# Two transformer layers on one core: engine queues ordered stage by stage, and operation by operation

## The reference

```
for l in (0, 1):
    x = x + attention_l(layernorm(x), ctx, ctx, mask_l)      # softmax over 128 keys, 16 heads
    h = layernorm(x)
    if l == 0:  x = x + bitlinear(silu(bitlinear(h, Wg)) * bitlinear(h, Wu), Wd)
    else:       x = x + sum over the 2 best experts e of w_e * (relu(h @ W1[e].T + b1[e]) @ W2[e].T + b2[e])
```

## Time and profile before

| | us |
|---|---|
| Median of 3 runs (lowest, highest) | 238.72 (238.11, 239.03) |
| The profiled execution | 239.16 |
| Its span | 237.3 |
| PE matmul busy, 2097 instructions | 201.5 |
| PE weight loads busy | 166.0 |
| DVE busy, 573 instructions | 169.5 |
| ACT busy, 377 instructions | 134.3 |
| POOL busy, 232 instructions | 110.6 |

### The profile page before, as it was taken

How to read it: one execution, slowest core, us unless ns; L and a number is a source line. 1 busy time by engine, 2 the same in 40 slices (tenths; PEclk the granted TensorE clock), 3 DMA queues, 4 the chain that set the end, 5 groups by cost and what they waited for, 6 DMA issues and landing times.

```text
span 237.3 us, 5951 instructions
## 1 busy us (share of the span) xinstructions
PE 201.5 (85%) x2097; PEld 166.0 (70%) x2114; DVE 169.5 (71%) x573; ACT 134.3 (57%) x377; POOL 110.6 (47%) x232
## 2 busy tenths in 40 slices
PE   0467299988675799898999999999899999999993
PEld 0245077866353577675779789897779979999992
DVE  1541974899999999999888998679756364625335
ACT  2242028685445465585959666567567738366560
POOL 6997022352475746423244562845262460482531
PEclk9999999999999689999999999999999999999998
DMA  6999044244003147040404002340400400000000
GB/s 203 356 397 201 1 88 41 53 90 91 0 3 62 28 88 91 0 91 15 82 0 76 15 4 38 64 91 11 91 0 3 91 12 4 0 14 11 14 0 22
DMA packets 39442, 15.09 MB, mean 64 GB/s; under 512 B 34163, under 2 KB 38515, under 8 KB 39158
## 3 DMA queue, kind: packets, MB, share of 16 engines
q1 hardware_dynamic: 38982, 14.00, 27.3%
q10 hardware_dynamic: 432, 0.72, 0.9%
HBM read 5.80 MB, written 0.52 MB: 27 GB/s over the span
## 4 chain that ended last, share of the span: by engine, by line
PE 49%; DVE 33%; DMA 4%; issue 4%; POOL 4%; SPq 2%; ACT 2%; DVEq 0%; ACTq 0%; POOLq 0%; another core or an unknown queue 0%
PE ps_B L705 11%; PE ps_A L720 10%; DVE mx L924 7%; PE ps_O L648 4%; PE ps_A L591 4%; PE ps_A L593 3%; PE ps_Q L637 3%; PE ps_B L606 3%; PE ps_B L608 3%; DMA wf_sb<-in_wd 3%; PE ps_P L628 2%; POOL yc L553 2%; DMA kblk<-kst 2%; DVE z L988 2%; PE ps_O L657 2%
## 5 line engine op out<-in xcount | busy, mean ns | idle before, releaser
L924 DVE TENSOR_REDUCE mx<-ps_A 128x4 f32<-128x512 f32 x64 | 41.9, 681 | 10.0 <-PE ps_A L593 9.5
L806 ACT ACTIVATE probs<-ps_B 128x512 f32<-128x512 f32 x64 | 36.9, 608 | 12.3 <-PE ps_B L608 11.9
L816 ACT ACTIVATE hid<-ps_B,b_sb 128x128 f32<-128x128 f32 x128 | 35.6, 383 | 12.7 <-PE ps_B L705 12.6
L591 PE MATMUL ps_A<-m_b,id_b 128*128 128x512 bf16 x64 | 25.9, 405 | 11.7 <-DVE mx L924 8.8
L705 PE MATMUL ps_B<-mxT,w_sb 128*128 128x128 f32 x256 | 33.5, 279 | 0.1
L720 PE MATMUL ps_A<-w_sb,hid 128*128 128x128 f32 x256 | 31.1, 275 | 0.4
L720 PEld LDWEIGHTS ps_A<-w_sb,hid 128*128 128x128 f32 x256 | 31.1, 192 | 0.6
L705 PEld LDWEIGHTS ps_B<-mxT,w_sb 128*128 128x128 f32 x256 | 30.6, 192 | 0.3 <-issue 0.2
L443 POOL TENSOR_SCALAR hv<-mv 128x1 f32<-128x1 f32 x32 | 7.3, 229 | 50.3 <-DVE mv L899 50.2
L553 POOL TENSOR_TENSOR yc<-yc 128x512 f32<-128x512 f32 (+2 forms) x21 | 17.2, 818 | 27.0 <-DVE yc L1052 25.9
L452 POOL TENSOR_SCALAR xh<-x_sb,mv,ry 128x128 f32<-128x128 f32 x32 | 26.1, 816 | 3.5
(11 more groups left out here) (128 smaller groups left out, 399.8 us busy)
## 6 DMA issues: line engine op xcount, KB each, us to landing
w_sb<-in_m1T SPq DMA_DIRECT2D x1, 1024.0 KB
w_sb<-in_m2T SPq DMA_DIRECT2D x1, 1024.0 KB
ctx_sb<-in_ctxT ACTq DMA_DIRECT2D x1, 512.0 KB, 5.0
m_i<-in_mask SPq DMA_DIRECT2D x1, 512.0 KB, 6.8
m0T_i<-in_mask0T SPq DMA_DIRECT2D x1, 512.0 KB, 7.5
out_y<-out_sb SPq DMA_DIRECT2D x8, 64.0 KB, 1.6
x_sb<-in_x SPq DMA_DIRECT2D x1, 448.0 KB, 5.5
wf_sb<-in_wg SPq DMA_DIRECT2D x1, 256.0 KB, 6.0
```

The lines of the kernel that those rows point to most:

```text
L591: pe.matmul(o[:, :].rearrange("p (h k) -> p h k", h=4), id_b[:, :], m, start=True, stop=False)
L806: ins = act.activation(probs[:, n % 2, 4 * i:4 * i + 4, :], psum("exp", n, i)[:, :].rearrange("p (h k) -> p h k", h=4), ACT.Exp, scale=ATT ...
L816: ins = act.activation(hid[:, b % 2, 4 * i + c, :], psum("z", b, i)[:, c * P:(c + 1) * P], ACT.Relu, bias=b1_sb[:, 4 * i + c:4 * i + c + 1])
L924: ins = dve.tensor_reduce(mx[:, n % 2, 4 * i:4 * i + 4], psum("max", n, i)[:, :].rearrange("p (h k) -> p h k", h=4), AX.X, ALU.max)
```

## The change

The plan orders operations where it ordered stages. Each helper's chain is cut into named steps (on DVE: st, ag, nm, rk, rq, m1, mr, m2, m3, rd, at, fs, fa, fn, q0 to qc, xr, xq, h0 to h3, hr, hq, lg to c5), each with a semaphore of its own. A step waits for those steps whose results or slots it needs, and between two steps of one unit the queue can hold steps of others. The plan's durations become pairs (`TIME`): the distance to the next step and the time to the end; a transpose of keys has 2.5 and 4.5. `START`, `BIAS` and two places in the unit order are new.

Keys and values are one product ("kv") that needs only the context, in bank X; the queries are another ("q"), in bank P. The 128x128 step of every layer norm moves from POOL to DVE (nm, fn). In the split of the maxima, the second part is computed from the maxima and the first part and no longer copied from the rest. The weights' sums (ws), product for the means (wm), three ternary steps for each of the three matrices (wa, wb, wc), the bias parts (five bp) and masks (mk, m1) are steps of their own. The loads: the context in two parts, keys' weights first; the feed-forward weights ahead of the mask of layer 1; a semaphore for each. POOL's clearing of all staging slots comes ahead of the first norm. The rest of the arithmetic and of the tiles stays.

```diff
-UNIT_ORDER = ((0, 0), (0, 1), (0, 2), (0, 3), (0, 4), (0, 5), (1, 0), (0, 6), (1, 1), (1, 2), (0, 7),
+UNIT_ORDER = ((0, 0), (0, 1), (0, 2), (0, 3), (0, 4), (0, 5), (0, 6), (1, 0), (0, 7), (1, 1), (1, 2),
               (1, 3), (1, 4), (1, 5), (1, 6), (1, 7))
 ATTENTION = (
-    ("pe.xT", 1, "pool.norm"),
+    ("dve.st", 1),
+    ("dve.ag", 1, "dve.st"),
+    ("pool.pw", 1, "dve.ag"),
+    ("dve.nm", 1, "pool.pw"),
+    ("pe.kv", 1),
+    ("act.kh", 1, "pe.kv"),
+    ("act.v", 1, "pe.kv"),
+    ("dve.rk", 1, "act.kh", "act.v"),
+    ("pool.km", 1, "dve.rk"),
+    ("pool.kl", 1, "pool.km"),
+    ("sp.ks", 1, "pool.kl"),
+    ("pe.xT", 1, "dve.nm"),
     ("act.xT", 1, "pe.xT"),
-    ("pe.qkv", 1, "act.xT"),
-    ("act.qkv", 1, "pe.qkv"),
-    ("dve.qkv", 1, "act.qkv"),
-    ("pool.low", 1, "dve.qkv"),
-    ("sp.ks", 1, "pool.low"),
-    ("pe.qs", 1, "pool.low"),
+    ("pe.q", 1, "act.xT"),
+    ("act.qh", 1, "pe.q"),
+    ("dve.rq", 1, "act.qh"),
+    ("pool.qm", 1, "dve.rq"),
+    ("pool.ql", 1, "pool.qm"),
+    ("pe.qs", 1, "pool.ql"),
...
+ONCE = (
+    ("dve.ws", 3),
+    ("pe.wm", 1, "dve.ws"),
+    ("dve.wm", 1, "pe.wm"),
+    ("dve.wa", 3, "dve.wm"),
+    ("dve.wb", 3, "dve.wa"),
+    ("dve.wc", 3, "dve.wb"),
+    ("pool.m1", 1),
+    ("dve.bp", 5),
 )
...
-LATENCY = 0.26
-LANDING = 3.5
+LATENCY = 0.1
+SAME = 0.03
 PATIENCE = 0.01
-START = (7, -55.6, 91.8, 80.2, 94.6, 137, 2.4, -27.2, -19.8, -42.4, 46, 26.4, 126.8, -60.8, 159.6, -19)
-
+START = (-36, -22, 2, -46, 42, 62, 14, 36, 63, 53, 102, 61, 36, 4, 44, -80)
...
+        def after(eng, step, u, i=None):
+
+            eng.wait_ge(done[step], u * counts[step] + (counts[step] if i is None else i + 1))
+
+        def ends(ins, step):
+            ins.then_inc(done[step], 1)
...
+            def power(k, b, step, u):
+
+                pool.tensor_scalar(hv[:, k, b, 0:1], mv[:, k, b, 1:2], EPS, None, ALU.add).then_inc(var_ready, 1)
+                small[0] += 1
+                pool.wait_ge(var_ready, small[0])
+                ends(pool.tensor_tensor(ry[:, k, b, :], hv[:, k, b, 0:1], half[:, :], ALU.pow), step)
...
+                if name == "nm":
+                    after(dve, "pool.pw", n)
+                    if n >= 2:
+                        after(dve, "pe.xT", n - 2)
+                    ends(dve.tensor_scalar(xh[:, n % 2, :], x_sb[:, b, :], mv[:, 2 * l, b, 0:1], ry[:, 2 * l, b, :],
+                                           ALU.subtract, ALU.mult), "dve.nm")
...
+                if name == "m2":
+                    st, m, rest = head_max(n)
+                    after(dve, "dve.m1", n)
+                    ends(dve.scalar_tensor_tensor(out=st[:, :, :, 1], in0=m, scalar=-1.0, in1=st[:, :, :, 0],
+                                                  op0=ALU.mult, op1=ALU.subtract), "dve.m2")
...
+                if name == "wa":
+                    after(dve, "dve.wm", 0)
+                    ends(dve.tensor_scalar(wf_sb[:, i, :], wf_sb[:, i, :], wf_inv[:, i:i + 1], ROUND,
+                                           ALU.mult, ALU.add), "dve.wa")
...
+                if name == "bp": bias_part(i)
```

More of the change, by code:

```diff
@@ L38 @@
 GROUPS = H // 2
-PAIR = 2 * DH
 PARTS = 6
@@ L130 @@
 )
[L132 to L146, removed]
-)
@@ L149 @@
[L149 to L157, removed]
@@ new lines, in _ @@
+                if name == "qs":
+                    after(pe, "pool.ql", n)
+                    stack("qs", n, ROWS)
+                if name == "max": maxima_scores(n, i)
+                if name == "qb":
+                    after(pe, "dve.m3", n)
+                    stack("qb", n, MROWS)
+                if name == "exp": shifted_scores(n, i)
+                if name == "pv":
+                    after(pe, "act.v", n)
+                    after(pe, "act.exp", n)
+                    wait_free(pe, "pv", n)
+                    if n == 0:
+                        pe.wait_ge(bank_zero, 1)
+                    o = psum("pv", n)
+                    for h in range(H):
+                        j = h % 4
+                        mm = pe.matmul(o[32 * j:32 * j + DH + 1, (h // 4) * P:(h // 4 + 1) * P],
+                                       v_sb[:, n % KSLOTS, h, :], probs[:, n % 2, h, :], start=True, stop=True)
+                    ends(mm, "pe.pv")
@@ new lines, in _ @@
+                if name == "oT":
+                    after(pe, "act.pv", n)
+                    wait_free(pe, "oT", n)
+                    o = psum("oT", n)
+                    for g in range(4):
+                        mm = pe.transpose(o[:, g * P:(g + 1) * P], oT_sb[:, n % 2, g * P:(g + 1) * P], ident)
+                    ends(mm, "pe.oT")
+                if name == "aT":
+                    after(pe, "dve.at", n)
+                    turn("aT", n, attn[:, n % 2, :, :].rearrange("p h d -> p (h d)"), ident)
@@ new lines, in _ @@
+                if name == "z":
+                    if b == 0 and i == 0:
+                        pe.wait_ge(s_moe, 80)
+                    if i == 0:
+                        after(pe, "act.mxT", b)
+                    wait_free(pe, "z", b, i)
+                    for c in range(4):
+                        mm = pe.matmul(psum("z", b, i)[:, c * P:(c + 1) * P], w1_sb[:, 4 * i + c, :], mxT[:, b % 2, :],
+                                       start=True, stop=True)
+                    ends(mm, "pe.z")
@@ new lines, in _ @@
+                if name == "y":
+                    if b == 0 and i == 0:
+                        after(pe, "dve.bp", 0)
+                        pe.wait_ge(ones_ready, 2)
+                    wait_free(pe, "y", b, i)
+                    o = psum("y", b, i)
+                    pe.matmul(o[:, :], rows3[:, :], b2_p[:, i * 512:(i + 1) * 512], start=True, stop=False)
+                    after(pe, "act.z", b, 2 * i + 1)
+                    for c in range(8 * i, 8 * i + 8):
+                        e = c // 2 - 4 * i
+                        mm = pe.matmul(o[:, e * P:(e + 1) * P], hid[:, b % 2, c, :], w2_sb[:, c, :],
+                                       start=False, stop=(c == 8 * i + 7))
+                    ends(mm, "pe.y")
```

1302 lines of the change are left out of this document (682 added, 620 removed).

## The result

The changed kernel takes 222.57 us (median of 4, 222.05 to 223.34), the kernel before 238.88 (median of 4, 238.11 to 239.15): a ratio of 0.9325, 95% interval 0.9284 to 0.9366. The gain is 16.3 us; 19.0 were forecast.

A forecast was written before the change was run, and what follows sets the result against it. Three stages were seen: a waiting start, a middle where DVE is fuller, an end where PE is. 237.3 - 6 - 12 - 1 = 218.3 us of span, plus 1.86 less 0.44 gives 219.7 us; range 206 to 234.

The forecast's parts named there:

- The middle: From 34 to 123 us, where DVE is the fuller engine: shrinks by 12 us, bounds 0 and 21.
- uncovered waits: DVE in the middle stage: 116 waits of 0.12 us, all covered by other units' steps, 13.9 us less.
- norm steps: Last step of each normalisation moves from POOL to DVE: some 15 in the middle, 3 us more, bounds 2 and 4.2.
- the bias block: Five bias steps run as one block from 69.60 us, then PE waits: splitting them gains 3, inside the middle's 12.
- the prediction's third rival: DVE's pitch doesn't fall, chained steps costing the same with or without waits between: 237 us, chance 0.05.
- The start: Before 34 us, where PE and DVE are idle half of the time: gain 6 us, bounds 1 and 8.
- the block that leaves the path: Start: nine ternary steps and the means, 4.2 and 0.7 us, done in DVE's idle time: 4.9 us gained.
- an earlier landing of the keys: Start: first key transpose lands at 20.3 us instead of 21.4, between 18.6 and 21.4: 1.1 us gained.
- The end: From 123 us, where PE is already full: gain 1 us from 2 us of pauses, bounds 0 and 2.
- Keys apart from queries: Keys and values in bank X, queries in P: cost 0, any gain inside the middle's 0 to 21.
- The rival "slower": Queues run in order and PE stands waiting for late key transposes, sixteen waits of 1.5 us: 243.7 us, chance 0.12.
- the marks that the prediction named: Signs in the new trace by stage: step distances, busy totals, transpose issue, PE waits, first expert product near 105 us.

The follow-up runs named there:

- e_stage: Changed kernel with the steps of each chain standing together again in VectorE's queue, all other queues unchanged: 246.47 us.
- e_blocks: Changed kernel with the nine ternary steps packed together and the five bias steps packed together in VectorE's queue: 228.54 us.
- e_hole: Changed kernel with the third weight sum, the product for the means, the means and nine ternary steps ahead of the first maximum: 221.46 us.
- e_early: Changed kernel with the five loads of expert weights issued behind the fifth key transpose, not ahead of the first: 217.24 us.
- e_early2: Changed kernel with the five loads of expert weights issued after the second key transpose, not ahead of the first: 216.92 us.
- k_tied: Changed kernel with keys and values of a unit computed only behind the transposed queries' input, all queues planned again: 235.56 us.
- k_stage: Changed kernel with the planner itself keeping the VectorE steps of a chain together, all five queues planned again: 242.94 us.
- k_pool: Changed kernel with both 128x128 norm steps back on GpSimd, queues planned again with a limit on how far key products run ahead: 239.26 us.
- e_both: Changed kernel with the edits of e_early2 and e_hole together: 219.5 us.
- e_twice: Changed kernel with each of the 32 norm steps done twice on VectorE, first into an unread spare tile, orders unchanged: 230.2 us.

## Why the prediction was right, and where it was not

**The middle: the length right, its split only in part.** 12 us were forecast: 10.9 less content on DVE (13.9 of uncovered waits less 3 of norm steps), and 1 less idle time. By the same PE prices as in the prediction, the pauses between 34 us and the first expert product went from 21 to 8.7 us: 12.3. The mechanism is there: 0.12 to 0.13 us from start to start per wait, in the rows of both kernels, and 12.9 us of DVE busy time that come back in e_stage. But the sum came out by two misses that offset each other. Between 34 us and the first expert product DVE's busy time fell from 78.9 to 72.9 us, by 6.0 and not by 10.9 (the stage doesn't hold quite the same work: some ternary steps are in it, and 35 "max" reductions instead of 39); its idle time fell from 10.1 to 2.7 us, by 7.4 and not by 1. That the length was hit this closely is luck. What filled the idle time, no run takes apart. One part is the bias block: in the kernel before PE waits 2.94 us behind it and is then busy 6.1 us in 6.8 us at half clock, both gone in the kernel after, and with the two blocks packed again it costs 6.0 us (e_blocks), where the prediction gave 3.

A norm step takes 0.36 (xh) or 0.40 us (fh), not 0.28, and is followed after 0.25 (28.09 to 28.34) instead of 0.2: 3.8 instead of 3, within its bounds. Chains packed again cost 20 to 24 us; the 12 are a net figure against a kernel whose queues were planned for its stages.

The Trainium skill ("VectorE: DVE Perf Modes", section "The DRAIN you can't avoid"), whose rule is the prediction's third rival, would have packing cost nothing. By the measurement it costs 23.9 us, of which 12.9 are on DVE itself. The measurement decides. The same section adds that a next operation that isn't held starts earlier, and with that the trace agrees: 0.06 to 0.13 us behind steps of 0.14 to 0.21.

**The start: one term right, one mis-sized.** Forecast 6 us (bounds 1 to 8): 4.9 for the block that leaves the path, 1.1 for an earlier landing of the keys. By the same prices PE had done 7.3 us of its work at 34 us before (counted from its instructions; the prediction has 8) and 9.4 after: 2 us. The 4.9 are there: the fourth "max" piece starts 7.8 us behind the first before (21.48 to 29.25) and 2.7 us after (23.43 to 26.08), 5.1 less. They didn't come as foreseen, by the nine steps filling DVE's idle time, for the third weight sum stands behind the first maxima in the queue; they came because the steps stand behind all four maxima. e_hole, where they do fill it, adds 1.1 us.

The term that failed is the landing: 20.3 forecast, between 18.6 and 21.4, and 23.4 measured (21.8 in the earliest execution with these loads and this order), so that 1.1 us of gain became 2 us of loss. Both of its bounds took SP's loads as issued when they were before, the last at 11.31. In the kernel after single issues took up to 1.33 us, the second of the two large expert loads went out at 11.75 instead of 9.56, and the last load at 13.35. The keys land 11.8 us behind that expert load before (21.4) and 11.6 after (23.3): ready 6 us earlier, they still waited for SP's loads. e_early and e_early2 show it: with the loads moved away the start gains 5.3 and 5.7 us more. Together with the 2 us that exceeds the forecast of 6, but by a change that wasn't made here.

**The end: right.** Gain 1 forecast; pauses between the first expert product and the last 21 us went from 2 to 1 us.

**What I had at nothing.** Keys apart from queries were costed at 0 with a gain inside the bounds. k_tied loses 13 us by tying them, but with a plan not fitted to the tie; what they are worth in a fitted one is open. Packed chains, tied keys and the norm on POOL cost 20, 13 and 17 us each alone, which can't be added up. My reading, argued and not shown, is that each breaks the same thing, a PE queue that always has another unit's work ready. The clock was at nothing too, outside the bias block: the kernel after has no stretch that its rows show at half clock, and e_stage, e_blocks, k_stage, k_tied and k_pool each have 6.8 us or more. The rival "slower" didn't come: no PE wait between 34 and 110 us is for a key transpose.

**Of the marks that the prediction named** these came true: small steps at 0.13 us or less, DVE busy 150 to 165 (162.5), POOL near 85 (88.2), the first transpose right behind the last load, no PE wait of 4.8 us behind the first maximum, the first expert product before 115 (109.6; 105 was named), PE full at the end. Not true: the mean before 18 us (30.44) and the first maximum at 21 to 22 (24.47).

**Open:** how much of k_pool's 16.7 us is the longer chain over POOL and how much a plan whose biases weren't fitted to it. Putting the norm back with all orders unchanged wasn't tried. Nor was a plan for stages, as in the kernel before, with newly fitted biases: how much of the 16.3 us is the finer grain and how much better fitted biases, the runs don't separate.

## What to carry to other kernels

Where an engine's trace shows steps that start later than the last one's duration, count these waits and look for work of another chain to put between them: the price per wait is read from two neighbouring rows, and packing them again on one queue alone shows on that engine's busy time that it is paid (12.9 us here), though not what a plan for packed chains would cost. Compare the granted clock of the variants as well: a pause can be paid a second time as slow matmuls behind it (e_blocks). Then look at what is queued ahead of the first transfer that the compute engines wait for: moving five loads of weights that are needed some 90 us later behind it gave 5.7 us, where reordering the compute of the start (e_hole) gave 1.1. An idle time is worth filling only with work that is shorter than it, and it may close once its cause is removed (e_both).

## What the runs showed of the hardware

The first key transpose, issued 2.4 us behind the second of two 1 MB weight loads on the same ring, took 9.3 us to its use, issued 5.0 us behind it 6.9 (kernel before), and issued ahead of both 6.3 (e_early2), with a median of 4.3 over the run. The issue of a load on SP took 0.35 to 0.56 us for most loads and up to 1.33 in the first 9 us of the kernel after (up to 0.93 before, 2.68 in e_hole). With the same loads in the same order the last one went out between 12.18 (e_twice) and 13.83 us (e_hole), so a difference of 1.5 us there says nothing of the order. A 128x128 fp32 scalar step with two per-partition operands took 0.36 to 0.40 us on DVE where the one-operand step took 0.28. A wait of PE for 2.82 us was followed by 10 us at a granted clock of 0.50 (e_blocks), one for 2.94 us by 6.8 us at 0.50 (kernel before).
